# Where three blocks of work stand in the order of a transformer tile: mask products, P times V, and the first key transposes

## The reference, cut to what matters

```python
for i in range(DEPTH):
    x = attn_layer(shift_tokens(x), Wqkv[i], q_scale[i], k_scale[i], Wo[i]) + x
    x = ffn_layer(shift_tokens(x), ln_g[i], ln_b[i], W1[i], b1[i], W2[i], b2[i]) + x
...
qkv = x @ Wqkv
q, k = rotary(l2norm(q) * qs), rotary(l2norm(k) * ksc)
...
sim = einsum('bhwie,bhwje->bhwij', q, keys_of_two_windows) * 8.0
sim = where(mask, -max, sim)
out = einsum('bhwij,bhwje->bhwie', softmax(sim), values_of_two_windows)
return out @ Wo
```

## Time and profile before

| | |
|---|---|
| median of 3 runs | 1634.21 us (1633.87 to 1636.32) |
| span of the profiled execution | 1634.9 us, 50862 instructions |
| busy share of the span | PE 98%, DVE 85%, PEld 84%, ACT 82%, POOL 81% |
| granted TensorE clock, mean | 0.994 |

### The profile page before, as it was taken

How to read it: one execution, slowest core, us unless ns; L and a number is a source line. 1 busy time by engine, 2 the same in 40 slices (tenths; PEclk the granted TensorE clock), 3 DMA queues, 4 the chain that set the end, 5 groups by cost and what they waited for, 6 DMA issues and landing times.

```text
span 1634.9 us, 50862 instructions
## 1 busy us (share of the span) xinstructions
PE 1595.9 (98%) x19920; PEld 1370.2 (84%) x19920; DVE 1395.7 (85%) x2021; ACT 1341.3 (82%) x2516; POOL 1321.6 (81%) x1278
## 2 busy tenths in 40 slices
PE   5999999999999999999999999999999999999997
PEld 3778888888888888888888888888888888888886
DVE  7888888888888888888888888888888899999975
ACT  5778888888888888888888888888888888888874
POOL 9888899888889888889888889888888777777741
PEclk8999999999999999999999999999999999999999
DMA  5234233333323344232344324244332332222231
GB/s 166 80 114 138 73 95 93 113 109 100 106 75 93 102 117 121 75 108 70 96 112 127 99 73 111 70 121 109 110 95 76 85 101 73 78 73 70 64 90 58
DMA packets 184872, 156.89 MB, mean 96 GB/s; under 512 B 111551, under 2 KB 156093, under 8 KB 184637
## 3 DMA queue, kind: packets, MB, share of 16 engines
q1 hardware_dynamic: 184636, 153.64, 33.6%
HBM read 27.56 MB, written 1.05 MB: 17 GB/s over the span
## 4 chain that ended last, share of the span: by engine, by line
PE 87%; ACT 4%; POOL 2%; DVE 2%; issue 2%; DMA 0%; SPq 0%; ACTq 0%; POOLq 0%; DVEq 0%
PE ps_pv L807 12%; PE ps_s L783 11%; PE ps_pv L826 10%; PE ps_tr L744 9%; PE ps_qn L719 9%; PE ps_qn L720 7%; PE ps_qn L721 7%; PE ps_tr L731 5%; PE ps_pv L816 3%; PE ps_qn L906 2%; PE ps_qn L907 2%; PE ps_s L766 2%; PE ps_qn L908 2%; PE ps_qn L893 1%; PE ps_pv L864 1%
## 5 line engine op out<-in xcount | busy, mean ns | idle before, releaser
L2032 POOL TENSOR_TENSOR qk<-qk,t 128x1024 f32<-128x1024 f32 x192 | 456.0, 2376 | 82.0 <-DVE qk L1550 81.4
L1547 DVE TENSOR_TENSOR t<-ps_qn,tab 128x512 f32<-128x512 f32 x384 | 264.3, 688 | 121.5 <-ACT sq L1145 109.9
L2044 POOL TENSOR_TENSOR qkr<-qk,rinv 128x1024 f32<-128x1024 f32 x192 | 361.5, 1903 | 8.0 <-POOL rinv L2024 0.8
L1132 ACT ACTIVATE pbd<-ps_tr 64x512 f32<-64x512 f32 x384 | 226.4, 590 | 55.3 <-PE ps_tr L731 51.7
L719 PE MATMUL ps_qn<-w_hi,xs_hi 128*128 128x512 f32 x576 | 260.9, 453 | 10.8 <-DVE qk L1550 8.1
L1550 DVE TENSOR_TENSOR qk<-ps_qn,tab 128x512 f32<-128x512 f32 x384 | 260.9, 679 | 0.0
L1145 ACT ACTIVATE sq<-ps_qn 128x512 f32<-128x512 f32 x384 | 228.8, 596 | 32.7 <-PE ps_qn L721 27.9
L1178 ACT ACTIVATE qbd<-ps_tr 64x512 f32<-64x512 f32 x384 | 227.3, 592 | 34.2 <-PE ps_tr L744 28.7
L720 PE MATMUL ps_qn<-w_lo,xs_hi 128*128 128x512 f32 x576 | 229.8, 399 | 0.0
L721 PE MATMUL ps_qn<-w_hi,xs_lo 128*128 128x512 f32 x576 | 229.2, 398 | 0.0
L1560 DVE TENSOR_REDUCE ss<-sq 128x32 f32<-128x2048 f32 x96 | 216.5, 2256 | 0.0
(11 more groups left out here) (177 smaller groups left out, 3178.7 us busy)
## 6 DMA issues: line engine op xcount, KB each, us to landing
v_own<-v_new SPq DMA_DIRECT2D x96, 512.0 KB, 3.3
v_back<-v_new SPq DMA_DIRECT2D x96, 384.0 KB, 3.5
v_back<-v_own SPq DMA_DIRECT2D x94, 128.0 KB, 2.3
kT<-kT SPq DMA_DIRECT2D x84, 128.0 KB, 2.7
w_raw<-in_Wqkv SPq DMA_DIRECT2D x18, 512.0 KB, 5.0
rot<-in_rot SPq DMA_DIRECT2D x48, 128.0 KB, 2.7
fx<-xmid SPq DMA_DIRECT2D x96, 64.0 KB, 2.1
xsh<-x SPq DMA_DIRECT2D x190, 32.0 KB, 2.6
```

What stands on the lines that cost most here:

```text
L1547: v.tensor_tensor(t2[:, part].rearrange("p (h s d) -> p h s d", s=2, d=DH // 2), swapped, tab[:, 2 * k + 1:2 * k + 2, :].rearrange("p o (s ...
L2032: g.tensor_tensor(qk[b][:, part], qk[b][:, part], t2[:, part], ALU.add).then_inc(added[b], 1)
L2044: g.tensor_tensor(qkr[b][:, part].rearrange("p (h d) -> p h d", d=DH), qk[b][:, part].rearrange("p (h d) -> p h d", d=DH), rinv[b][:, k * ...
```

## The change

On TensorE, the mask products move from between the two parts of P times V to directly in front of the scores. The transposes of keys 2 move from the middle of the half to in front of P times V; those of keys 3 stay. On ACT, the copy of keys 2 out of PSUM moves in front of the two copies of P times V. SP, DVE and POOL, and the drain after the last step, are as they were. The order in which banks are taken is the same.

```diff
                     qkv(i, b, (0, 1))
                     if (i.n, b) == (1, 1):
                         transpose_pair(1)
+                    transpose_qk(i, b, 2)
                     probs_v(i, b, 0)
-                    mask(i, b)
                     probs_v(i, b, 1)
                     qkv(i, b, (2, 3))
...
                     if b == 0:
                         ffn_down(i)
-                        transpose_keys(i, b)
+                        transpose_qk(i, b, 3)
                         ffn_centre(i)
...
                         out_projection(i, b)
                         rec_gate_projection(i, b)
-                        transpose_keys(i, b)
+                        transpose_qk(i, b, 3)
...
                         qkv(i, b, (4, 5))
                         ffn_broadcast(i)
                         ffn_up(i, 2)
+                    mask(i, b)
                     scores(i, b, 0)
                     scores(i, b, 1)
@@ ACT, half(i, b)
+                    evac_k(i, b, 0)
                     evac_pv(i, b, 0)
                     evac_pv(i, b, 1)
                     square(i, b, 2)
...
                     rec_gelu(i, b)
-                    evac_k(i, b, 0)
                     evac_k(i, b, 1)
```

More of the change, by code:

```diff
@@ L746, in transpose_qk @@
                     last.then_inc(tr_full[bank], 1)
-                def transpose_keys(i, b):
-                    transpose_qk(i, b, 2)
-                    transpose_qk(i, b, 3)
                 def transpose_queries(i, b):
```

## The result

The changed kernel takes 1746.84 us (median of 4 runs, 1743.35 to 1749.21) against 1635.05 us for the kernel before (1633.87 to 1636.32): a ratio of 1.0683, with a 95% interval of 1.0668 to 1.0699. That is 112 us slower. The forecast was 1724, in a range of 1688 to 1756, and slower.

A forecast was written before the change was run, and what follows sets the result against it. TensorE, busy 98%, bounds the kernel before; after the change the carry's landing paces halves b = 0. 37 plain steps at +1.87 and 8 recurrent at +2.67 give 90 us, so 1724 us, range 1688 to 1756.

The forecast's parts named there:

- ACT stands at its new copy in 45 halves b = 0, some 110 us together.: At ACT's early copy into `kT`: some 45 waits for the carry DMA, 2 to 3.5 us each, some 110 us together.
- TensorE loses it at `ffn_down` and `ffn_centre`.: In halves b = 0, TensorE waits about 1.5 us for ACT's `oT` copy, then about 0.6 us for DVE's rotation.
- The landing of a half b = 0 hangs on DVE's scaling at the end of the half before: On SP: the carry queues behind `fx` DMAs awaiting DVE's scaling, 3.2 us before its issue, so earlier TensorE gains are lost.
- A landing 2.8 us after the issue.: Key carry into `kT`, b = 0: issued at 822.55, landed at 825.35, taking the median transfer time of 2.80 us.
- 3.5 us from the landing to `ffn_centre`: In step 26, b = 0: carry lands at 825.35, delayed copies, square and rotation follow, and `ffn_centre` starts at 828.85.
- The rest of the step.: Plain step +1.87 us: 1.7 late at `ffn_centre` in b = 0, plus 0.32 for the mask, less 0.15 in b = 1.
- In halves b = 1 the order gives 0.15 us.: P times V is 0.46 us shorter, but chunk 4 needs a bank DVE frees, so some 0.15 us come through.
- rival 3: No wait for the carry, TensorE's order alone counts: 0.14 us for each of 94 halves, 13 us, 1621; chance 0.06.
- Recurrent steps +2.67.: At `rec_hidden` in 8 recurrent steps: full 2.5 us lateness of the squares, plus 0.32, less 0.15, +2.67 us each.
- That is 0.46 us less per half: On TensorE: taking the mask out of P times V cuts the stretch from 2.48 to 2.02 us per half.

The follow-up runs named there:

- The carry first: The changed kernel with SP issuing the key carry first in each half, ahead of the `fx` DMAs: 1632.24 us, ratio 0.9991 to the kernel before.
- the early copy in halves b = 1 alone: The changed kernel with ACT's copy of keys 2 put back behind the exponentials in halves b = 0: 1632.67 us, ratio 0.9987 to the kernel before.
- The run with the mask alone: The kernel before with only the mask products moved in front of the scores, transposes and ACT's copies unmoved: 1659.63 us, ratio 1.0151.
- that with both masks: The kernel before with a second pair of mask products in front of the scores, the old pair kept within P times V: 1659.30 us, ratio 1.0153.
- the carry in between: The changed kernel with SP issuing the key carry right behind `shift_xmid`, ahead of the rotary table: 1655.60 us, ratio 1.0130 to the kernel before.

## Why the prediction was right, and where its sum was off

- *ACT stands at its new copy in 45 halves b = 0, some 110 us together.* Right: 45 times, 112.3 us. The carry first takes the whole loss away, the early copy in halves b = 1 alone has none of it.
- *TensorE loses it at `ffn_down` and `ffn_centre`.* Right. The waits are 53.9 us in 43 halves and 25.4 in 39, so 1.25 and 0.65 us each, against 1.5 and 0.6. Two waits of the start, 3.7 and 4.6 us at 98 and 134 us, are in the second; in the plain steps at full clock it is 0.46. P times V is one stretch of 2.02 us in the chain (861.04), as forecast.
- *The landing of a half b = 0 hangs on DVE's scaling at the end of the half before, so TensorE's gains ahead of it are lost.* Right; the chain goes that way, and the plain steps show it as a landing plus a constant.
- *A landing 2.8 us after the issue.* This is the term that was mis-sized. In the plain steps of the changed kernel the landings for stream 0 take 3.02 us in the mean. In the kernel before they take 2.82, so that the trace I had could not tell; why they are longer now is open. The other term that was off is one that the sum doesn't have, the clock: 0.22 us per plain step.
- *3.5 us from the landing to `ffn_centre`* (825.35 to 828.85). Measured at full clock, 3.63 us (847.10 to 850.73; this is a first tile of a layer, and the plain steps have 3.62). In the half at the lower clock of the chain above it is 4.57 (881.79 to 886.36), so 0.94 of the 1.68 us came through by which `ffn_down` and the transposes were longer there.
- *The rest of the step.* Without the landing, the forecast's step is 31.79 + 1.87 - 2.80 = 30.86 us, and 30.86 is measured. That it fits to a hundredth is luck in part. 3.63 for 3.50 is 0.13 too little, and from `ffn_centre` to the next issue the forecast has 27.36 (30.86 - 3.50), where 27.22 is measured (850.73 to 877.95): 0.14 too much.
- *In halves b = 1 the order gives 0.15 us.* The term is not measured by itself in the changed kernel. With the carry first the whole order is worth 1.5 us of the 13 that rival 3 forecast. Part of what swallowed it was the gate product, as the forecast said: moving 0.25 us of DVE's work out of its way gave 5 us more (1632.24 to 1626.85). What holds back the other 6 is not shown.
- *Recurrent steps +2.67.* Measured +2.57.
- *"That is 0.46 us less per half"* failed as a statement on the kernel before, though in the forecast's sum it carried only 0.15. The stretch 1.08 + 0.32 + 1.08 was read as TensorE's work alone. Its second part was released by ACT's copy, with no time in hand, and the mask was the filler. The run with the mask alone (+26 us) and that with both masks (+25 us) show it. Rival 3, an order that gains 13 us by itself, could not have come true even with a carry in time.

The sum was 90 us and 112 were measured. 18 of the 22 are in the plain steps, (2.36 - 1.87) x 37. The 0.49 of one step are 0.22 of longer landings (3.02 for 2.80), 0.22 of half clock and 0.05 from the one step at 569.64. Over 37 steps that is 8 us from the landings, 8 from the clock and 2 from that step, if the other 8 plain steps were like the 29 that were read. The rest lies outside the plain steps and was not followed up.

## What to carry to other kernels

When an instruction on an in-order engine is moved ahead, list every semaphore it waits for, and read from the trace when the slowest of them comes, not the one that the move is about. The copy's producer was made early; its other wait, a DMA that had been late once in the whole trace, and by 0.7 us, was not there in time, and stood in front of five instructions.

A long busy stretch on the engine that sets the pace can hold a wait that a filler covers. Before such a filler is moved, look for what releases the instruction behind it: if that ended just before, the filler was free. And a change that is worth nothing by itself can be worth something with the next bottleneck moved, as the mask's move was here: +26 us alone, -12 us with the transposes in its place.

## What the hardware showed that was not expected

- After TensorE had been idle for 2.1 us ahead of `ffn_down`, its granted clock was at half (1.2 GHz) for 3.42 us, beginning when it had just taken up work again. Between 62 and 1560 us this happened in 8 of the 45 halves with a wait of ACT for the carry: in six after a wait of 1.75 to 2.33 us at `ffn_down`, and in two around waits of 3.7 and 4.6 us at `ffn_centre`. It didn't always: waits of 1.77 and 2.15 us at `ffn_down` (711.61 and 338.48) had no such stretch behind them. With waits of at most 0.9 us at `ffn_down` (the carry in between) it never happened between 62 and 1560 us. In the plain steps a stretch of 3.4 us at half clock went with 0.96 to 1.13 us more of the step.
- The key carry took 3.6 us in the median from issue to landing when it was issued first in a half, against 2.8 at its old place, for the same 128 KB. The kernel before shows the same with the carry first (3.6), so it is the place of the issue and not the order on TensorE or ACT.
- With the carry issued at its old place, the landings of stream 0 spread from 2.6 to 4.2 us in the plain steps of the changed kernel, and since they set the pace, the steps spread with them.
